# Attention on eight cores: the running sum of the exponentials on one engine, and each block's normalisation spread over the next block's steps

## The reference

```python
q, k = apply_rope(q, cos, sin), apply_rope(k, cos, sin)
k = jnp.repeat(k, groups, axis=1); v = jnp.repeat(v, groups, axis=1)
scores = jnp.einsum('bhqd,bhkd->bhqk', q, k) * scale
attn = jax.nn.softmax(scores, axis=-1)
out = jnp.einsum('bhqk,bhkd->bhqd', attn, v)
...
x = _layernorm(x + attention(x)); x = _layernorm(x + ffn(x))
```

## Time and profile before

| what | us |
|---|---|
| timed runs | 11,433.92, 11,314.64, 11,007.96 (median 11,314.64) |
| the profiled execution | 10,832.11 |
| its span on the slowest core (core 3) | 10,830.6 |
| spans of the eight cores | 10,781.4 to 10,830.6 |
| attention, from its first score matmul to the end of its last multiply | 3762 |

### The profile page before, as it was taken

How to read it: one execution, slowest core, us unless ns; L and a number is a source line. 1 busy time by engine, 2 the same in 40 slices (tenths; PEclk the granted TensorE clock), 3 DMA queues, 4 the chain that set the end, 5 groups by cost and what they waited for, 6 DMA issues and landing times.

```text
span 10830.6 us, 90059 instructions; the slowest of 8 cores (10781.4 to 10830.6 us)
## 1 busy us (share of the span) xinstructions
PE 7110.6 (66%) x29224; PEld 2826.4 (26%) x29224; DVE 4317.1 (40%) x3297; ACT 3473.0 (32%) x3523; POOL 3384.4 (31%) x1545
## 2 busy tenths in 40 slices
PE   3444443446666666666666555688888888888863
PEld 1222221211111112112111222233333333333321
DVE  1222222147777777777777332101111121111045
ACT  1111111136666656666666211021121121121121
POOL 1111110037777777777777200000000000000000
PEclk8777776679989999999998877799999999999975
DMA  9999985220000000000000210121221221222121
GB/s 143 147 149 161 157 142 103 78 63 2 6 14 11 6 3 22 3 6 7 3 3 3 56 47 24 22 33 30 36 32 30 34 32 31 35 32 31 33 33 47
DMA packets 908300, 500.95 MB, mean 46 GB/s; under 512 B 794560, under 2 KB 831552, under 8 KB 903232
## 3 DMA queue, kind: packets, MB, share of 16 engines
q0 software_dynamic: 489552, 251.72, 17.7%
q1 hardware_dynamic: 418288, 243.45, 8.1%
HBM read 545.43 MB, written 125.83 MB: 62 GB/s over the span
## 4 chain that ended last, share of the span: by engine, by line
PE 45%; ACT 20%; DMA 10%; DVE 10%; POOL 8%; issue 4%; another core or an unknown queue 1%; SPq 1%; ACTq 0%; DVEq 0%; POOLq 0%; PEldq 0%
ACT p_expS L546 14%; PE pA L943 10%; PE pA L929 10%; POOL p_sumacc L515 8%; PE pB L978 5%; PE pC L978 5%; PE pA L525 4%; DMA p_xbf<-xfull 3%; DMA p_tbs<-rks 3%; PE pB L693 2%; PE pA L360 2%; DMA p_tbs<-rqs 2%; PE pB L307 1%; DMA wf_sp<-p_wtmp 1%; ACT p_act L937 1%
## 5 line engine op out<-in xcount | busy, mean ns | idle before, releaser
L515 POOL TENSOR_TENSOR p_sumacc<-p_sumacc,p_expS 128x1024 f32<-128x1024 f32 x960 | 2751.0, 2866 | 222.6 <-ACT p_expS L546 96.0
L512 DVE TENSOR_TENSOR p_sumacc<-p_sumacc,p_expS 128x1024 f32<-128x1024 f32 x960 | 2487.7, 2591 | 461.5 <-ACT p_expS L546 461.5
L546 ACT ACTIVATE p_expS<-pA,cexpb 128x1024 bf16<-128x1024 f32 x2048 | 2284.8, 1116 | 822.9 <-PE pA L525 694.9
L525 PE MATMUL pA<-p_qtb,p_ktb 128*128 128x512 bf16 x4096 | 1281.2, 397 | 986.1 <-ACT p_expS L546 949.7
L943 PE MATMUL pA<-h_sb,p_wgu 128*128 128x512 bf16 x4608 | 1083.7, 399 | 166.0 <-ACT p_act L937 166.0
L929 PE MATMUL pA<-h_sb,p_wgu 128*128 128x512 bf16 x4608 | 1054.2, 391 | 139.4 <-ACT p_ut L953 139.4
L957 DVE TENSOR_TENSOR p_act<-p_act,p_ut 128x2048 bf16<-128x2048 bf16 x72 | 88.2, 1225 | 2476.3 <-ACT p_ut L953 2476.3
L525 PEld LDWEIGHTS pA<-p_qtb,p_ktb 128*128 128x128 bf16 x4096 | 283.6, 99 | 1986.9 <-issue 1981.6
L922 POOL DMA_DIRECT2D p_wgu<-wf_sp x72 | 83.0, 1153 | 2233.0 <-PE pA L943 2233.0
L943 PEld LDWEIGHTS pA<-h_sb,p_wgu 128*128 128x128 bf16 x4608 | 464.9, 102 | 784.8 <-issue 303.9
L929 PEld LDWEIGHTS pA<-h_sb,p_wgu 128*128 128x128 bf16 x4608 | 457.2, 100 | 735.8 <-issue 235.8
(11 more groups left out here) (186 smaller groups left out, 5815.3 us busy)
## 6 DMA issues: line engine op xcount, KB each, us to landing
wf_sp<-p_wtmp SPq DMA_DIRECT2D x144, 512.0 KB, 5.2
p_wgu<-wf_sp POOLq DMA_DIRECT2D x144, 512.0 KB, 6.7
p_xbf<-xfull POOLq DMA_DIRECT2D x64, 512.0 KB, 10.8
p_wtmp<-wg POOLq DMA_DIRECT2D x64, 512.0 KB, 12.4
p_wtmp<-wu POOLq DMA_DIRECT2D x64, 512.0 KB, 11.7
p_wdt<-wd POOLq DMA_DIRECT2D x128, 256.0 KB, 4.4
p_tbc<-rkc SPq DMA_DIRECT2D x64, 256.0 KB, 7.5
p_tbs<-rks SPq DMA_DIRECT2D x64, 256.0 KB, 8.9
```

The lines of the kernel that those rows point to most:

```text
L512: P.op("vector", lambda e, eb=eb: e.tensor_tensor(sumacc[:, 0:1024], sumacc[:, 0:1024], eb[:, 0:1024], ALU.add), waits=W(exph_ms[0]))
L515: P.op("gpsimd", lambda e, eb=eb: e.tensor_tensor(sumacc[:, 1024:2048], sumacc[:, 1024:2048], eb[:, 1024:2048], ALU.add), waits=W(exph_ms[1]))
L525: P.op("tensor", lambda e, gb=gb, kc=kc, k2=k2, ss=ss, hi=hi, qt=qt: e.matmul(pA[:, hi * 1024 + k2 * 512: hi * 1024 + (k2 + 1) * 512], ktb ...
L546: P.op("scalar", lambda e, kk=kk, hi=hi: e.activation(expS[kk % 2][:, hi * 1024:(hi + 1) * 1024], pA[:, hi * 1024:(hi + 1) * 1024], AF.Exp ...
```

## The change

Two things are changed, both in attention. First, GpSimd no longer adds: VectorE adds both heads' halves in one 128x2048 instruction (a 128x2048 copy in the first step), and this add waits for both exponentials of the step. Second, the block's epilogue becomes five pieces that a list, `pend_epi`, holds and that the next block's steps append at `kk` = 1, 3, 5, 7 and 9: `s1` the sums over partitions, `s2` the copies and reciprocals, `s3` the spreading matmuls, `s4` the two copies of the spread rows, `s5` the multiplies and the stores. Only the last value matmuls, the last add and the two copies of the accumulators stay at the block's end, and these copies now wait for the value matmuls alone. The last block's pieces are appended after the loops.

```diff
+                    while pend_epi and kk >= pend_epi[0][0]:
+                        pend_epi.pop(0)[1]()
                     if kk >= 1:
                         if first:
-                            P.op("vector", lambda e, eb=eb: e.tensor_copy(
-                                sumacc[:, 0:1024], eb[:, 0:1024]),
-                                waits=W(exph_ms[0], sumacc_free))
-                            P.op("gpsimd", lambda e, eb=eb: e.tensor_copy(
-                                sumacc[:, 1024:2048], eb[:, 1024:2048]),
-                                waits=W(exph_ms[1], sumacc_free))
+                            P.op("vector", lambda e, eb=eb: e.tensor_copy(
+                                sumacc[:], eb[:]),
+                                waits=W(exph_ms[0], exph_ms[1], sumacc_free[0]))
                         else:
-                            P.op("vector", lambda e, eb=eb: e.tensor_tensor(
-                                sumacc[:, 0:1024], sumacc[:, 0:1024],
-                                eb[:, 0:1024], ALU.add), waits=W(exph_ms[0]))
-                            P.op("gpsimd", lambda e, eb=eb: e.tensor_tensor(
-                                sumacc[:, 1024:2048], sumacc[:, 1024:2048],
-                                eb[:, 1024:2048], ALU.add), waits=W(exph_ms[1]))
+                            P.op("vector", lambda e, eb=eb: e.tensor_tensor(
+                                sumacc[:], sumacc[:], eb[:], ALU.add),
+                                waits=W(exph_ms[0], exph_ms[1]))
...
-                        expS_free[(kk - 1) % 2] = [av_ms[0], av_ms[1],
-                                                   sum_ms_v, sum_ms_p]
+                        expS_free[(kk - 1) % 2] = [av_ms[0], av_ms[1], sum_ms_v]
...
                 for hi in range(2):
                     P.op("scalar", lambda e, hi=hi: e.copy(
                         av_f[hi][:], pB[:] if hi == 0 else pC[:]),
-                        waits=([reps] + W(avf_free[hi])), inc="sSE")
-                    pBC_free2[hi] = P.ms("sSE")
+                        waits=[av_ms[hi]] + W(avf_free[hi]), inc="sSE")
+                    avf_in[hi] = P.ms("sSE")
+                    pBC_free2[hi] = avf_in[hi]
+                pend_epi.extend(mk_epi(sum_done_v, avf_in[0], avf_in[1],
+                                       h0, h1, qt))
...
+    while pend_epi:
+        pend_epi.pop(0)[1]()
```

More of the change, by code:

```diff
@@ L480, in build_nc, with s3, s4, s5 @@
     exph_ms = [None, None]
-    pDE_free = None
-    sumacc_free = None
+    pDE_free = [None]
+    sumacc_free = [None]
     pBC_free2 = [None, None]
+    pend_epi = []
+    def mk_epi(sum_done_v, avf0, avf1, h0, h1, qt):
+        box = {'avf': [avf0, avf1]}
+        def s1():
+            for hi in range(2):
+                for k2 in range(2):
+                    P.op("tensor", lambda e, hi=hi, k2=k2: e.matmul(
+                        (pD if hi == 0 else pE)[0:1, :], ones_cf[:],
+                        sumacc[:, hi * 1024 + k2 * 512: hi * 1024 + (k2 + 1) * 512],
+                        start=(k2 == 0), stop=(k2 == 1)),
+                        waits=([sum_done_v] + W(pDE_free[0]))
+                              if (hi == 0 and k2 == 0) else (),
+                        inc="sPE" if (hi == 1 and k2 == 1) else None)
+            box['sums'] = P.ms("sPE")
+            sumacc_free[0] = box['sums']
+        def s2():
+            P.op("vector", lambda e: e.tensor_copy(d_row[0][:], pD[0:1, :]),
+                 waits=[box['sums']] + W(drow_free[0], drow_free[1]))
+            P.op("vector", lambda e: e.tensor_copy(d_row[1][:], pE[0:1, :]))
+            P.op("vector", lambda e: e.reciprocal(d_row[0][:], d_row[0][:]))
+            P.op("vector", lambda e: e.reciprocal(d_row[1][:], d_row[1][:]))
+            box['rcp'] = P.ms("sVE")
+        def s3():
+            P.op("tensor", lambda e: e.matmul(
+                pD[:], onesr[:], d_row[0][:], start=True, stop=True),
+                waits=W(box['rcp']))
+            P.op("tensor", lambda e: e.matmul(
+                pE[:], onesr[:], d_row[1][:], start=True, stop=True),
+                inc="sPE")
+            box['reps'] = P.ms("sPE")
+            drow_free[0] = box['reps']
+            drow_free[1] = box['reps']
+        def s4():
+            for hi in range(2):
+                P.op("scalar", lambda e, hi=hi: e.copy(
+                    rep_f[hi][:], (pD if hi == 0 else pE)[:]),
+                    waits=([box['reps']] if hi == 0 else []) + W(repf_free[hi]),
+                    inc="sSE")
+            box['evs'] = P.ms("sSE")
+            pDE_free[0] = box['evs']
+        def s5():
+            for hi, hh in enumerate((h0, h1)):
+                slot = (qt * 2 + hi) % 4
+                P.op("vector", lambda e, hi=hi, slot=slot: e.tensor_tensor(
+                    att_t[slot][:], av_f[hi][:], rep_f[hi][:], ALU.mult),
+                    waits=[box['evs'], box['avf'][hi]] + W(att_free[slot]))
+                nrm = P.ms("sVE")
+                avf_free[hi] = nrm
+                repf_free[hi] = nrm
+                att_free[slot] = P.dma("sync",
+                    lambda e, hh=hh, qt=qt, slot=slot: e.dma_start(
+                        out=at_sp[hh][:, qt * 512:(qt + 1) * 512],
+                        in_=att_t[slot][:]),
+                    f"dAt{slot}", waits=[nrm])
+        return [(1, s1), (3, s2), (5, s3), (7, s4), (9, s5)]
@@ L574, in build_nc @@
-                sum_done_p = P.ms("sPO")
-                expS_free[1] = [av_ms[0], av_ms[1], sum_done_v, sum_done_p]
-                for hi in range(2):
-                    for k2 in range(2):
-                        w = ()
-                        if hi == 0 and k2 == 0:
-                            w = [sum_done_v] + W(pDE_free)
-                        elif hi == 1 and k2 == 0:
-                            w = [sum_done_p]
-                        P.op("tensor", lambda e, hi=hi, k2=k2: e.matmul(
-                            (pD if hi == 0 else pE)[0:1, :], ones_cf[:],
-                            sumacc[:, hi * 1024 + k2 * 512: hi * 1024 + (k2 + 1) * 512],
-                            start=(k2 == 0), stop=(k2 == 1)),
-                            waits=w,
-                            inc="sPE" if (hi == 1 and k2 == 1) else None)
```

47 lines of the change are left out of this document (4 added, 43 removed).

## The result

The change made the kernel faster: its time is 0.9355 of the time before (95% interval 0.9329 to 0.9381), 6.5% less. The profiled execution went from 10,832.1 to 10,126.1 us; 10,142 had been forecast for it. The median of ten runs went from 11,143.2 to 10,674.5 us, against a forecast of 10,420. The medians lie so far above the profiled executions, and their own ratio is 0.958, because 7 of the 10 executions of either kernel took 2 to 6% longer, in the changed kernel with a granted TensorE clock of 0.77 to 0.85 on the cores of one or both dies in place of 0.866; the ratio of 0.9355 leaves these out.

What follows compares the result with a forecast made beforehand. GpSimd's adds were taken to pace attention's steps at 3.06 us, with a 21 us serial block end as second cost. Savings of 648, 37 and 5 us gave 10,142 profiled; plus 280, 10,420 us median, range 10,080 to 10,790.

Steps and rivals of the forecast that it cites:

- The wide add: 128x2048 add on VectorE in attention: 2.29 us with GpSimd out of the stage, bounds 2.13 and 5.2.
- The step: Attention key step: the loop over two buffers of exponentials sets 2.44 us, 78.1 us for 32 steps.
- Sums ahead of step 1's scores: Sums in TensorE's queue delay step 1's scores and exponential in the next block: 3.1 us lost.
- Copies and reciprocals: On VectorE ahead of step 2's add, delaying step 4's exponential: 8.4 us lost whole.
- Spreading matmuls: At step 5 on TensorE, they fall into the hole the reciprocals leave: cost 0.
- The clock: TensorE holds full clock through the boundary but halves behind step 4's hole: 1.4 us a block, bounds 0 and 7.
- The sum: Attention blocks: 95.2 us against 116.8, 648 us saved over 30 inner blocks, 690 together; profiled execution 10,142 us.
- A: Rival: the add's slack hides the reciprocals on VectorE; block 81 us, median 10,010 us; chance 0.04.
- B: Rival: TensorE stays at 1.2 GHz for the whole block; block about 123 us, median 11,310 us; chance 0.05.
- C: Rival: VectorE's wide add costs more than two lone halves, 2.65 us; median 10,710 us; chance 0.06.
- D: Rival: VectorE's 2.71 us is its own price, so the add takes 5.26 us; median 13,120 us; chance 0.04.
- The median: Whole-kernel runs: median 280 us above the profiled execution's 10,142, within 176 to 482, giving 10,420 us.

Runs made afterwards that it cites:

- two-row sums: Changed kernel with both heads' sums in two rows of one PSUM tile, so one copy and one reciprocal replace two of each: 9,986 us, 91.8 us a block.

## Why the prediction was right

*The wide add.* Forecast 2.29 us, measured 2.292, the mean of 957. The ground for it, that GpSimd is what slows VectorE, was argued from one row of 1.23 us; the run with GpSimd adding beside shows it.

*The step.* Forecast 2.44, measured 2.467, set by the loop over two buffers (the third buffer gave 2.41). The two hand-overs in it took 0.17 and 0.15 us where 0.16 and 0.11 had been read, 0.05 more over two steps. Over 32 steps that is 0.8 us.

*The pieces.* Sums ahead of step 1's scores: forecast 3.1, measured a wait of 3.07. Copies and reciprocals: 8.4, measured 8.53, and shown exposed by leaving the reciprocals out. Copies on ScalarE 1.3 and multiplies on VectorE 1.6: measured 1.35 (from 3064.25 to the next exponential at 3065.60) and a wait of 1.67, of which 0.20 is there anyway. Spreading matmuls: 0, in the hole.

*The clock.* Forecast 1.4 us, with the hole moved and not gone. The two steps behind it take 5.83 us (3056.01 to 3061.84) instead of 4.93, so 0.9; the run without reciprocals puts it at some 0.7, where its expectation had given it 2. The clock holding through the boundary came out as forecast, but it was not safe: with three buffers, where TensorE idles 2.18 us there instead of 1.01, it fell in the middle of the sums.

*The sum.* With the gaps that every step has taken off the waits, 78.9 + 1.5 (copies at the boundary) + 3.0 + 8.3 + 1.35 + 1.5 + 0.9 = 95.5 us; 95.5 measured, the mean of 30, and 95.2 forecast. The step was 0.8 us too short and the clock's price 0.5 too high, so part of the closeness is luck. Attention was to save 690 us and saved 696: the 30 inner blocks 659 (648 forecast, from one block of 116.8 where the mean is 117.5), the first block 34 (37) and the last 2.5 (5). The profiled execution came out 16 us under the forecast; 10 of these lie outside attention, where nothing had been forecast.

*The rivals.* A (reciprocals hidden) falls with the wait of 8.53. B (half clock throughout) with the granted clock of 0.94 in the stage. C with the 2292 ns, D with the run beside GpSimd.

*The median.* This is the term that failed. The prediction put 280 us between the profiled execution and the median, "nearer the lower since two of the four executions lie there"; over ten runs it was 548. Four executions were too few for the middle of ten, and the profiled one among them was the lowest. The kernel's part of the forecast isn't touched by it, and the time, 254 us above the forecast, lies inside the stated range mostly because its upper end allows for executions 600 us above the profiled one.

## What to carry to other kernels

Before two engines share an elementwise job in SBUF, look for a row in which one of them works alone: here one engine did both halves in 2.29 us, where two side by side took 2.71 and 2.92. Spreading an epilogue over the next block's steps hides nothing by itself: each piece stands in a queue ahead of work that the pace depends on, so its length must fit into the slack that the buffers give, and a piece that waits must not stand where its input is still being made. More buffers and shorter pieces belong together: a third buffer alone brought 31 us, and cutting the pieces with two buffers cost some 40 against the two-row sums uncut, while four buffers and small pieces, with the shorter reciprocal and a second accumulator, brought the kernel from 10,112 to 9,700. Which of these could be left out again, and whether three buffers would do, was not tried, except that two buffers don't.
